# First batch by halves of heads, q/k stacks gathered by term, in a one-core hybrid transformer kernel

## What is computed

```python
q, k, v = jnp.split(_layernorm(x) @ w_attn + b_attn, 3, axis=-1)     # 32 heads of 16
scores = jnp.einsum('bqhd,bkhd->bhqk', q, k) * SCALE
scores = jnp.where(causal[None, None], scores + slopes * rel, -jnp.inf)
attn = jax.nn.softmax(scores, axis=-1)
x = x + jnp.einsum('bhqk,bkhd->bqhd', attn, v).reshape(B, S, HIDDEN) @ w_proj + b_proj
x = x + _L0_ffn_ref(...)      # three experts, two of them picked
x = x + _L0_attn_b_ref(...)   # gated MLP with a top-k mask
x = x + _L0_ffn_ref(...)
```

## Time and profile before

| | before |
|---|---|
| median of 3 executions | 681.93 us (681.78 to 682.07) |
| the profiled execution: time / span | 681.57 us / 679.8 us |
| TensorE (PE) matmul busy | 641.1 us, 94% |
| VectorE (DVE) busy | 483.0 us, 71% |
| ScalarE (ACT) busy | 343.7 us, 51% |
| GpSimd (POOL) busy | 92.0 us, 14% |
| DMA moved, mean | 52.15 MB, 77 GB/s |
| TensorE clock granted | 0.9 or more of full in all 40 slices |

### The profile page before, as it was taken

The page is one execution under the profiler, slowest core; times in us unless marked ns, Lnnn a source line. Parts: engine busy times, 40 slices in busy tenths (PEclk is TensorE's granted clock), DMA queues, the critical chain, the costliest instruction groups (busy, mean ns, idle before and its releaser), DMA issues.

```text
span 679.8 us, 10305 instructions
## 1 busy us (share of the span) xinstructions
PE 641.1 (94%) x3848; PEld 487.2 (72%) x3848; DVE 483.0 (71%) x921; ACT 343.7 (51%) x539; POOL 92.0 (14%) x185
## 2 busy tenths in 40 slices
PE   4878999999998999999999899999999999999997
PEld 4856678679676677887788576766857665788776
DVE  6755585796589889887697656365374898778556
ACT  5213544613633774522479997476483915434221
POOL 4411002102100121101042010000100350000000
PEclk9999999999999999999999999999999999999999
DMA  8395503322744331000161000000003106000000
GB/s 282 110 264 173 157 32 97 117 70 73 241 128 146 119 121 47 0 1 1 49 225 61 1 0 1 0 1 0 1 0 114 74 7 225 2 32 16 15 32 32
DMA packets 31908, 52.15 MB, mean 77 GB/s; under 512 B 3449, under 2 KB 17148, under 8 KB 30303
## 3 DMA queue, kind: packets, MB, share of 16 engines
q1 hardware_dynamic: 31282, 49.84, 22.6%
q10 hardware_dynamic: 576, 1.64, 1.0%
HBM read 42.87 MB, written 8.40 MB: 75 GB/s over the span
## 4 chain that ended last, share of the span: by engine, by line
PE 79%; DVE 12%; ACT 4%; DMA 1%; issue 1%; ACTq 1%; POOL 1%; SPq 0%; DVEq 0%; POOLq 0%
PE ps L2031 14%; PE ps L1900 13%; PE ps L1867 13%; PE ps L2100 10%; PE ps L1730 5%; DVE nmax L1099 3%; PE ps L1808 3%; PE ps L1746 2%; PE ps L1876 2%; PE ps L1798 2%; PE ps L1710 2%; DVE nmax L1096 2%; ACT sign_junk L988 1%; PE ps L1821 1%; PE ps L2089 1%
## 5 line engine op out<-in xcount | busy, mean ns | idle before, releaser
L2100 PE MATMUL ps<-wdT,prodT 128*128 128x512 f32 (+1 forms) x176 | 76.9, 592 | 0.0
L817 ACT ACTIVATE probsT<-ps 128x1536 f32<-128x1536 f32 x32 | 46.2, 1450 | 30.2 <-PE ps L1798 30.0
L2100 PEld LDWEIGHTS ps<-wdT,prodT 128*128 128x128 f32 (+1 forms) x176 | 32.8, 190 | 38.3 <-issue 38.3
L857 ACT ACTIVATE funs<-ps 128x512 f32<-128x512 f32 x16 | 9.5, 596 | 90.4 <-PE ps L1869 78.7
L683 POOL TENSOR_SCALAR ln_spread<-ln_moments 128x1 f32<-128x1 f32 x24 | 7.5, 311 | 272.1 <-DVE ln_moments L1171 271.9
L1633 DVE COPY prodT<-ps 128x512 f32<-128x512 f32 (+1 forms) x24 | 13.7, 599 | 41.3 <-PE ps L2089 41.0
L1177 DVE SCALAR_TENSOR_TENSOR junk<-x_sb,gate_row 128x512 f32<-128x512 f32 x48 | 41.2, 858 | 1.0
L1448 DVE SCALAR_TENSOR_TENSOR x_sb<-b_row,coef,x_sb 128x512 f32<-128x512 f32 x48 | 38.0, 792 | 1.8
L1099 DVE TENSOR_REDUCE nmax<-ps 128x4 f32<-128x1024 f32 x32 | 38.9, 1215 | 0.0
L988 ACT ACTIVATE sign_junk<-mlp_size_next,minus_guess 128x1376 bf16<-128x1376 f32 x24 | 34.6, 1443 | 0.8
L988 ACT ACTIVATE sign_junk<-mlp_size_main,minus_guess 128x1376 bf16<-128x1376 f32 x24 | 34.6, 1442 | 0.7
(11 more groups left out here) (302 smaller groups left out, 1726.4 us busy)
## 6 DMA issues: line engine op xcount, KB each, us to landing
cuts<-parts SPq DMA_DIRECT2D x16, 384.0 KB, 2.8
qst<-cuts SPq DMA_DIRECT2D x48, 128.0 KB, 2.6
w_first_raw<-in_L_ffn_w SPq DMA_DIRECT2D x6, 1024.0 KB, 7.6
w_second_raw<-in_L_ffn_w SPq DMA_DIRECT2D x6, 1024.0 KB, 8.5
kst<-cuts SPq DMA_DIRECT2D x36, 128.0 KB, 2.8
wqkv_raw<-in_L_attn_a_w_attn SPq DMA_DIRECT2D x3, 1024.0 KB, 8.0
wdT<-in_L_attn_b_w_down SPq DMA_DIRECT2D x1, 2560.0 KB, 9.9
wg_raw<-in_L_attn_b_w_gate SPq DMA_DIRECT2D x1, 2048.0 KB, 8.4
```

The costliest lines, as they stand in the source:

```text
L817: nc.scalar.activation(probsT[:, g % 2, :].rearrange("p (k n) -> p k n", k=3), slot[g % 2], ACT.Exp).then_inc(exp_ok.sem, 1)
L2100: last = nc.tensor.matmul(ps[:, Y_BANK, :], prodT[0:m, c, :], wdT[0:m, c, :], start=(c == 0), stop=(c == IC - 1))
```

## The change

1. `cuts` is replaced by two DRAM tensors. `q_cuts` holds q already repeated in the order of the six terms, `k_cuts` the three parts of k. A half's write is now three DMAs for q (its part 0 three times, part 1 twice, part 2 once, by `TERM_RUNS`; 768 KB) and one for k (384 KB): four issues and 1152 KB where there were two and 768 KB.
2. The stack's rows are ordered by term (row 16 t + d), not by d (row t + 6 d). A half is gathered by one DMA of 96 rows for q and three of 48, 32 and 16 rows for k, 8 KB a row: 4 issues where there were 12, the same 1536 KB.
3. Batch 0 goes by halves: f = 0, 1, 2, 3 on all engines. SyncE writes half 0, waits for `cuts_out[0]`, gathers q of half 0, then the same for half 1. ScalarE's queue sends the gathers of k of both halves, after its last `second_part` as before; the second three wait for `cuts_out[1]`.
4. GpSimd's first `cut` moves ahead of batch 1's layer norm.
5. The turned rows of even and odd batches have buffers of their own (`even_rowsT_*`, `odd_rowsT_*`), and batch 1's rows go through PSUM banks 0 and 1. So TensorE turns batch 1's rows before `value(0, ...)`, and `turned_part(1, 1)` moves from ahead of the scores to behind `scores(0, 1)`; VectorE's `residue(1, 0)` and `residue(1, 1)` move from ahead of the maxima to behind groups 1 and 3.
6. VectorE's four operations `cut_biases` move from the start to just ahead of the maxima; the bias DMAs on SyncE move behind the gathers of batch 0.

```diff
+TERM_RUNS = [(0, 3, 0), (3, 2, 1), (5, 1, 2)]
-        cuts = nc.dram_tensor("cuts", (2, 2, 3, D // 2, S), BF16, kind="Internal").ap()
+        q_cuts = nc.dram_tensor("q_cuts", (2, len(TERMS), P, 2 * S), BF16, kind="Internal").ap()
+        k_cuts = nc.dram_tensor("k_cuts", (2, 3, P, 2 * S), BF16, kind="Internal").ap()
+        def write_side(eng, b, half, side):
+            need(eng, part3, b, 2 * half + side + 1)
+            if side == 1:
+                eng.dma_start(k_cuts[half].rearrange("m p n -> p m n"),
+                              parts[:, 1, half].rearrange("p m g t -> p m (g t)")).then_inc(cuts_out[half].sem, 16)
+            else:
+                for t, n, part in TERM_RUNS:
+                    eng.dma_start(q_cuts[half, t:t + n].rearrange("m p n -> p m n"),
+                                  parts[:, 0, half, part].rearrange("p g t -> p (g t)").unsqueeze(1)
+                                  .broadcast_to([P, n, 2 * S])
+                                  ).then_inc(cuts_out[half].sem, 16)
         def send_rows(eng, b, half, side):
-            for t, term in enumerate(TERMS):
-                eng.dma_start(stack[t:TROWS:len(TERMS), hs, :],
-                              cuts[side, half, term[side]].rearrange("(d h) t -> d h t", d=HD)
+            if side == 0:
+                eng.dma_start(qst[0:TROWS, hs, :].rearrange("r h t -> r (h t)"),
+                              q_cuts[half].rearrange("m (d h) n -> (m d) (h n)", d=HD)
                               ).then_inc(scat[half].sem, 16)
+            else:
+                for t, n, _ in TERM_RUNS:
+                    eng.dma_start(kst[t * HD:(t + n) * HD, hs, :].rearrange("r h t -> r (h t)"),
+                                  k_cuts[half, 0:n].rearrange("m (d h) n -> (m d) (h n)", d=HD)
+                                  ).then_inc(scat[half].sem, 16)
...
+            for half in range(2):
+                for side in range(2):
+                    write_side(sp, 0, half, side)
+                need(sp, cuts_out[half], 0, 16 * WRITES)
+                send_rows(sp, 0, half, 0)
-            write_cuts(0, 0)
-            write_cuts(0, 1)
-            gather(0, 0, (0,))
-            gather(0, 1, (0,))
...
+            cut(0, (0,))
             ln(1)
-            cut(0)
+            cut(0, (1, 2, 3))
...
-            need(act, cuts_out[0], 0, 16 * 2)
-            send_rows(act, 0, 0, 1)
-            need(act, cuts_out[1], 0, 16 * 2)
-            send_rows(act, 0, 1, 1)
+            for half in range(2):
+                need(act, cuts_out[half], 0, 16 * WRITES)
+                send_rows(act, 0, half, 1)
```

More of the change, by code:

```diff
@@ L515, in row_banks @@
         def row_banks(b):
-            return first_rows if b == 0 else work
+            return first_rows if b <= 1 else work
         def row_bank(n):
@@ L553, in write_cuts, with gather @@
                 for side in range(2):
-                    need(sp, part3, b, place(b, 2 * half + side) + 1)
-                    sp.dma_start(cuts[side, half].rearrange("m (g p) t -> p (m g) t", p=P),
-                                 parts[:, side, half].rearrange("p m g t -> p (m g) t")
-                                 ).then_inc(cuts_out[half].sem, 16)
-            def gather(b, half, sides=range(2)):
+                    write_side(sp, b, half, side)
+            def gather(b, half):
                 need(sp, sT_ps, b - 1, (half + 1) * GHALF)
-                need(sp, cuts_out[half], b, 16 * 2)
-                for side in sides:
+                need(sp, cuts_out[half], b, 16 * WRITES)
+                for side in range(2):
                     send_rows(sp, b, half, side)
@@ L779, in first_part @@
                 side, pair = f % 2, f // 2
[L780 to L781 removed]
+                need(act, cuts_out[pair], b - 1, 16 * WRITES)
+                need(act, tr_ps, b, f + 1)
                 if b == 0 and f == 0:
@@ L1244, in steady, with first @@
                     residue(b + 1, 1)
+            def first(g):
+                if g == 1:
+                    residue(1, 0)
+                elif g == 3:
+                    residue(1, 1)
             for b in range(B - 1):
-                maxima(b, lambda g: steady(b, g) if b >= 1 else None)
+                maxima(b, first if b == 0 else lambda g: steady(b, g))
                 residue(b + 1, 2)
@@ L1709, in value @@
                     for c in range(KC):
-                        last = nc.tensor.matmul(work[j], rows[:, c, at_j], weight[:, 2, c, :],
+                        last = nc.tensor.matmul(work[j], rows[b % 2][:, c, at_j], weight[:, 2, c, :],
                                                 start=(i == 0 and c == 0), stop=(i == 2 and c == KC - 1))
```

116 lines of the change are left out of this document (54 added, 62 removed).

## The result

| | before | changed |
|---|---|---|
| median | 682.00 us (6 runs, 681.78 to 683.65) | 685.07 us (6 runs, 684.09 to 686.81) |
| profiled execution: time / span | 681.57 / 679.8 us | 685.49 / 683.7 us |
| maxima of batch 0 end | 57.28 us | 60.67 us |
| second pass begins | 62.56 us | 65.86 us |
| DMA moved | 52.15 MB | 55.29 MB |

What follows compares the result with a forecast made beforehand. The prediction took the end of batch 0's maxima (57.28 us) as the bound: of 4.7 us won at the first scores, 2.1 remain after the wait for half 1, so 681.93 - 2.1 = 679.8 us, range 678.1 to 682.9.

Steps and rivals of the forecast that it cites:

- The start of half 0: Batch 0: GpSimd's blocked cut ends at 24.4, the write lands at 27.2 and q's gather goes out, 3.8 us earlier.
- k's gathers: Half 0 on ScalarE's queue: start at 29.5 (29.2 to 30.3) behind its last second_part, 1.5 us earlier than 30.98.
- The first block: 2.75 MB of DMA from 28.1 to 38.0 or 38.6, including k's write of half 1; second gathers issued 38.5 or 39.1.
- The first scores: TensorE, batch 0: start at 36.5, 4.7 us earlier, with k's half 0 landing between 35.5 and 38.
- The second block: Half 1's gathers: 1.57 MB at 277 or 233 GB/s, 5.7 or 6.8 us, landed at 45.7 or 47.6.
- the round trip: Between the DMA blocks: half 1's gathers wait for k's write to land; data resume at 39.4 or 40.0.
- Rival C: k's gathers into adjacent rows run slower, at 98 GB/s: group 4 at 52.7, 2.5 us slower, 684.4; chance 0.16 with other losses.
- From half 1 to the end of the maxima: Scores take 1.3 us, so group 4's maxima begin at 47.0 to 48.9, against 50.24; gain taken as 2.1 us.
- The residues under the cover: VectorE's two batch 1 residues, 1.76 us, are covered by the wait for half 1 ahead of group 4.
- ScalarE behind its gathers: Part 0 of batch 1 comes at 40.9 to 41.8, making residue(1, 0) wait 0.7 us, inside the same cover.
- The later batches: Batches 1 to 3: four writes and fewer gathers change nothing on the path; 0.3 us allowed either way.
- The order as such: Batch 0 by halves, with gathers going out earlier: the forecast gain of 2.1 us at group 4's maxima.

Runs made afterwards that it cites:

- e2: Changed kernel with k's six terms each written out and gathered by one DMA of 96 rows, as q's are: 687.55 us, ratio 1.0071.
- e1: Changed kernel with SyncE's bulk loads held back until the gathers of both halves have landed: 686.20 us, ratio 1.0053.
- e3: Changed kernel's order and halves, but with the old tensor, writes and gathers of the kernel before: 682.36 us, ratio 0.9995.
- e11: Changed kernel with 12 and 22 spare mask matmuls filling TensorE's two waits for batch 0's gathers: 684.87 us, ratio 1.0037.
- e5: Changed kernel with turned_part(1, 1) moved into TensorE's long wait, behind scores(0, 3): 685.01 us, ratio 1.0037.
- e8: Old copies in halves, half 1's writes among half 0's gathers, SyncE sending all half 1, batch 1's residues and turned part ahead of the maxima: 680.02 us.
- e14: e8 with half 1's last three k gathers on ScalarE, and half 1's q and k writes behind half 0's third and sixth q gathers: 681.79 us.

## Why the prediction was wrong

- **The start of half 0: right.** The blocked `cut` ended at 24.30 against 24.4, q's gather went out at 26.98 against 27.2; this is the row of GpSimd, where I expected VectorE's weight cut to hold it:

```profile
21.81 2.49 POOL L690 TENSOR_TENSOR parts<-resid,parts 128x512 bf16<-128x512 f32 x1 [0.57 <-ACT parts L806]
```

- **k's gathers started at 28.16, not 29.5.** It did no visible harm.
- **The first block: right** on what it was to give, the landing of k's write: 39.05 (issued at 30.05, 9.0 us to landing), against 38.5 to 39.1, at 281 GB/s from 32 to 38. The first scores came at 37.85, not 36.5, within the 35.5 to 38 that I had given k's landing; which transfers held them I did not test. The wait for half 1 covers this.
- **The second block: the step that failed.** I let 1.57 MB move at 277 or 233 GB/s and landed it at 46.6; it moved at 178 to 203 and landed at 50.6. It went out 0.3 us behind the middle of what I had said and needed 11.5 us from issue to scores, where I had given it 7.8. By the runs, 1.4 of these 3.7 are k's blocks (11.5 against e2's 10.1) and 0.85 the bulk loads that I had not counted (e1). The remaining 1.45 is what is left over, if the loads cost the same everywhere, and was not measured by itself: whole or spread rows, loads included, needed 10.1 as well (e2; e3: 48.63 - 38.50), so I had them too fast too. I took the upper rate from a stretch in which writes were mixed in. The hole ahead of the block is not the error: the share of 0.11 from 38 to 40 us is the round trip that I had in the sum (first block over at 38.0 or 38.6, data again from 39.4 or 40.0). The later of my two landings has a slip besides: 46.8 and 0.5 give 47.3, not 47.6.
- **Rival C is what came**, at 0.16, in kind: group 4 was to begin at 52.7 and did at 52.94, for 684.4 us; it is 685.07. I had set it aside since k's largest block has 48 rows. Its price was 4.8 us of landing for a rate of 98; what k's blocks cost was 1.4. That its numbers fit is luck: loads, a block slower than I had it and the clock made up the rest. The Trainium skill's port map (SBUF — State Buffer, on the DMA port swizzle), which I had worked out to 1.6 us in the prediction and then left out of the sum, is close to the 1.4 between the changed kernel and e2.
- **From half 1 to the end of the maxima: a term that I put at nothing, 1.7 us.** Scores to maxima took 52.94 - 50.59 = 2.35, not 1.3, and the last four groups 7.73, where they took 7.04 before: the clock at 0.50. I did not ask what a wait of 5 us does to the engine that waits. With the clock at 1.00 both come back, to 52.13 - 50.83 = 1.30 and 7.04 in e11, and to 51.55 - 50.25 = 1.30 and 7.04 in e5.
- **The residues under the cover, ScalarE behind its gathers: right.** ScalarE took up part 0 of batch 1 at 40.53 (40.9 to 41.8 forecast), and VectorE, both residues done, still waited 4.41 us.
- **The later batches: right.** TensorE's waits for the maxima's DMA behind the first stage are as before, and the 3.3 us at 65.86 are carried on to the end (span +3.9).
- **The order as such** was to win 2.1 us and wins nothing with old copies: e3 starts half 1's scores at 48.63, where they started at 48.74. Its block goes out at 38.50 behind the hole, and needs 10.1 us. Without the hole, and with batch 1's residues and turned part back in their old places, it wins 2.4 (e8); the run that brings the hole back wins nothing (e14).
